# Adding the output-projection bias on GpSimd in pieces of one row block instead of one instruction

## What is computed

```python
x = x + attn(_layernorm(x))            # ... y @ Wo.T + bo
x = x + xattn(_layernorm(x), ctx)      # ... out @ W_out.T + b_out
x = x + ffn(_layernorm(x))             # fake-quantized silu(gate) * up, down
```

## Time and profile before

| | us |
|---|---|
| median of 3 runs | 990.71 (989.15 to 991.78) |
| the profiled execution, its own time | 986.81 |
| its span in the trace | 985.1 |
| POOL busy | 313.9 (32% of the span) |
| the nine bias instructions of line 679 | 36.4 of those |

### The profile page before, as it was taken

How to read it: one execution, slowest core, us unless ns; L and a number is a source line. 1 busy time by engine, 2 the same in 40 slices (tenths; PEclk the granted TensorE clock), 3 DMA queues, 4 the chain that set the end, 5 groups by cost and what they waited for, 6 DMA issues and landing times. The chain is left out here.

```text
span 985.1 us, 17246 instructions
## 1 busy us (share of the span) xinstructions
PE 899.3 (91%) x6003; PEld 440.0 (45%) x6018; DVE 710.8 (72%) x1467; ACT 601.1 (61%) x1118; POOL 313.9 (32%) x348
## 2 busy tenths in 40 slices
PE   4788999999999989999999999999999998988976
PEld 2433443455544534464446343554444454543344
DVE  3889866768766783777777928777674568778977
ACT  2335577746576577447675775456788624637974
POOL 1351135330431218413431165313512122203723
PEclk9979999999999999999999999999999999999999
DMA  5340111335222142101220313202210243115009
GB/s 164 108 124 17 56 58 53 76 60 82 82 77 73 43 146 76 55 17 56 92 88 17 126 45 99 63 31 82 87 49 2 86 150 100 37 38 171 1 9 184
DMA packets 83568, 73.42 MB, mean 75 GB/s; under 512 B 19244, under 2 KB 79788, under 8 KB 83484
## 3 DMA queue, kind: packets, MB, share of 16 engines
q1 hardware_dynamic: 75772, 66.17, 22.2%
q0 software_dynamic: 4256, 3.21, 2.6%
q10 hardware_dynamic: 3456, 2.94, 1.0%
HBM read 19.81 MB, written 13.13 MB: 33 GB/s over the span
## 5 line engine op out<-in xcount | busy, mean ns | idle before, releaser
L767 ACT ACTIVATE probs<-psum 128x512 f32<-128x512 f32 (+1 forms) x608 | 314.6, 577 | 179.5 <-PE psum L962 176.6
L1136 DVE CUSTOM_DVE_ANT_0 junk<-psum,mask 128x640 bf16<-128x640 f32 (+3 forms) x256 | 253.4, 1022 | 59.4 <-PE psum L926 57.2
L684 POOL TENSOR_SCALAR_AFFINE_SELECT probs<-probs 128x512 f32<-128x512 f32 x128 | 81.6, 640 | 391.5 <-ACT probs L767 391.2
L962 PE MATMUL psum<-q_stack,k_stack 98*128 98x512 bf16 (+3 forms) x768 | 188.0, 331 | 6.7 <-DMA q_stack<-max_rows 2.6
L987 PE MATMUL psum<-probs,v_sb 128*17 128x512 f32 (+3 forms) x1536 | 158.9, 492 | 3.8 <-POOL probs L684 3.4
L1132 DVE TENSOR_REDUCE rowmax<-psum 128x4 f32<-128x512 f32 (+2 forms) x96 | 97.3, 1045 | 62.9 <-PE psum L920 62.5
L926 PE MATMUL psum<-k_stack,q_stack 96*128 96x512 bf16 (+3 forms) x512 | 128.7, 344 | 5.8 <-DVE rowmax L1136 4.5
L962 PEld LDWEIGHTS psum<-q_stack,k_stack 98*128 98x128 bf16 x768 | 62.7, 98 | 136.6 <-ACT probs L767 80.9
L886 PE MATMUL psum<-xnT,wT 128*128 128x512 f32 x192 | 90.8, 604 | 0.6 <-ACT xnT L732 0.5
L811 PE MATMUL psum<-wT,xnT 128*128 128x256 f32 x384 | 87.6, 385 | 0.4 <-ACT xnT L732 0.3
L811 PEld LDWEIGHTS psum<-wT,xnT 128*128 128x128 f32 x384 | 73.3, 193 | 12.6 <-ACT xnT L732 1.2
(11 more groups left out here) (180 smaller groups left out, 1242.7 us busy)
## 6 DMA issues: line engine op xcount, KB each, us to landing
q_stack<-q_parts SPq DMA_DIRECT2D x192, 64.0 KB, 2.6
k_stack<-k_parts SPq DMA_DIRECT2D x192, 64.0 KB, 2.6
xq_stack<-xq_parts SPq DMA_DIRECT2D x168, 64.0 KB, 2.6
xn<-in_x SPq DMA_DIRECT2D x8, 512.0 KB, 5.0
res<-in_x SPq DMA_DIRECT2D x4, 1024.0 KB, 6.8
out<-res SPq DMA_DIRECT2D x8, 512.0 KB, 2.9
normT_hbm<-xnT SPq DMA_DIRECT2D x6, 512.0 KB, 3.9
xf<-normT_hbm SPq DMA_DIRECT2D x6, 512.0 KB, 3.7
```

Of the source, the lines that this page charges most:

```text
L684: nc.gpsimd.affine_select(out=tile, in_=tile, compare_op=ALU.is_ge, fill=0.0, base=0, pattern=[[0, GH], [1, P]], channel_multiplier=-1).th ...
L767: nc.scalar.activation(probs[n % 2][:, heads * k:heads * k + heads, 0:cols], bank_a(s)[:, 0:heads * cols].rearrange("p (h n) -> p h n", h= ...
L962: last = nc.tensor.matmul(bank[:, cols * n:cols * n + cols], k_stack[:, slot, h, P * j:P * j + P], q_stack[:, slot, half, h, q0 - HALF * h ...
L1136: nc.vector.tensor_tensor_reduce(out=junk[D_STEPS.place(s) % 2][:, 0:keys], in0=bank_d(s)[:, 0:keys], in1=m.mask[:, T - keys:T], scale=1.0 ...
```

## The change

POOL's one `tensor_tensor` for a `bias` step becomes a loop over its row blocks, one instruction of 128x256 each: eight where the step covers the batch, four in the two steps of batch 3. Only the last one of a step raises `biased`. There is no wait between the pieces. What is added, the tiles and the order of the steps stay.

```diff
                     bias = m.bias_f[(1, 3)[layer]][:, :].unsqueeze(1).to_broadcast([P, 4 * len(halves(part)), C])
-                    nc.gpsimd.tensor_tensor(rows, rows, bias, ALU.add).then_inc(biased, 1)
+
+                    for t in range(4 * len(halves(part))):
+                        last = nc.gpsimd.tensor_tensor(rows[:, t, :], rows[:, t, :], bias[:, t, :], ALU.add)
+                    last.then_inc(biased, 1)
```

## The result

The changed kernel is slower: 996.78 us median of 20 runs (992.22 to 1001.77) against 991.91 of 20 runs of the kernel before (986.33 to 998.04), ratio 1.0041, 95% interval 1.0024 to 1.0058 (the quotient of the two medians is 1.0049, within it). The profiled execution took 1001.77 us, at the slow end of its 20 runs, its span 1000.0. The forecast was 1.6 us less and the range ended at 993.6.

The account below looks back on a forecast made before the run. PE was busy 91% of the span, DVE 72%, POOL 32%, so POOL's work counts only through who waits. Terms -0.4 - 1.2 + 0 = -1.6 us gave 989.1 us, range 987.2 to 993.6.

Parts of the forecast that it names:

- The price of a piece: POOL's bias adds: 736 ns for 256 columns, eight pieces 5.54 us, POOL about 8 us busier.
- Nobody waits for POOL: Behind all nine biases, the next users of POOL's work have enough slack for its longer steps: cost 0.
- One link gets through at each boundary: Behind the first bias, eight linked DVE instructions pass eight POOL pieces, one for each piece: gain 0.4 us.
- The first stall: DVE line 1052 beside the bias of 70.75 us, 4.90 us long: -0.4 us forecast.
- the second: DVE line 1151 at 851.84 us beside the last two biases, 2.33 us long: PE gets back 1.2 us.
- rival 1: POOL doesn't let go between pieces: +1.0 at the first place, +0.85 at the last, sum +1.9, 992.6 us; chance 0.25.
- the trace agrees: Shared port of DVE and POOL: whoever starts first holds it for the whole instruction; 4.90 us against 4.51.
- rival 2: As rival 1, and TensorE's clock falls once more behind the first bias, 1.7 us: sum +3.6, 994.3 us; chance 0.08.
- Rival 3: Links hardly held by pieces: -2.1 us at the first bias, -1.2 at the last two, sum -3.3, 987.4; chance 0.12.
- The base: Median of the three runs before, 3.9 us above the profiled execution of 986.81, from which the 1.6 was taken.

Follow-up runs that it names:

- The middle alone: Against the kernel before, pieces in the six middle bias steps only, the first and the last two whole: ratio 1.0010.
- the unread matmuls: Changed kernel plus matmuls whose results nobody reads, put into TensorE's waits behind the two held DVE instructions: 1.0016 to the kernel before; that kernel filled likewise: 1.0004.
- the moved kernels: Against the kernel before, first and last bias start later, away from the DVE links: 0.9937 with whole biases, 0.9956 with pieces.
- the half pieces: Each piece of the change cut once more, 16 of 128x128 for a batch, no wait between: 1.0065 to the kernel before.

## Why the prediction was wrong, step by step

*The price of a piece*: 736 ns forecast, 721 measured; a train of eight 5.54 us forecast, 5.48 to 5.51 measured; POOL 8 us busier forecast, 7.7 by the groups. Right.

*Nobody waits for POOL*: right as far as the runs tell. The middle alone gives 1.0010 (0.9984 to 1.0035), and the stretches around its biases are as long as before (88.4 us).

*One link gets through at each boundary*: this is the step that failed. The first stall grew by 0.97 us (5.87 for 4.90, PE idle 2.90 for 1.91) where -0.4 was forecast, the second by 0.82 (3.15 for 2.33, PE idle 2.03 for 1.20) where -1.2 was. Not one of the seven boundaries was open. The mistake was to read from rows 6 how POOL's next instruction takes the port: there, nothing was queued on POOL. The row that showed a queued one was in rows 3, and the prediction used it only for rival 1: line 1052, issued 0.36 us ahead of the bias, lost against it. Its sizes, +1.0 and +0.85, are those measured. It should have had the larger chance, since every piece but the first is queued and nothing showed DVE getting in between two adds in succession. That such a hold would pass on to the time of its stage was right: 0.9 and 0.8 us.
The Trainium skill (GPSIMD Engine Reference, Instruction dispatch) says that GpSimd's cores go on to the next instruction with no barrier; the traces agree, as the trains have no gap (eight pieces of 721 ns take 5.48 us). The Trainium skill (SBUF — State Buffer, Who interferes with whom) has the port held for one whole instruction; here the 5.87 us show it held for a whole row of queued ones, and the measurement decides. The prediction's "the trace agrees" covered only the length of the hold: by the recorded starts the link, at 70.39, was ahead of the bias, at 70.75, and yet it was the one held.

*And the clock*: rival 2 put one fall more, 1.7 us, at a chance of 0.08. Nine traces have the pieces queued in the first step, and all nine have half clock in stage 2: 0.8 us with the unread matmuls, 1.7 to 5.4 in the others. Of the eight traces in which the first hold is as before or gone, seven have none; the exception is the one of the last two steps only (6.8). The price was 1.3 to 1.6 us in the change, 20.0 to between 21.3 and 21.6. "The 1.91 us of idling there now cost no clock" was true, and said nothing about 2.90.
Over all runs the change has a mean clock of 0.9796 (44 runs), the kernel before 0.9820 (126). The share of the time at half level is twice what the mean clock lacks to 1; that is 40.7 against 35.8 us. A microsecond at half level costs about half a microsecond at most (stage 3 of the kernel before took 13.5 us with 3.4 at half level and 11.9 with none): at most 2.4. With the holds, 0.97 + 0.82 + 2.4 = 4.2; measured 4.1 in the first comparison and 4.7 and 5.1 in the two others. That the sum fits doesn't prove the clock's part. Within the 126 runs of the unchanged kernel a microsecond more at half level goes with only 0.37 us more of time, and at that price the sum is 3.6. And the kernel with pieces in the first step has the half clock of stage 2 in both its traces, but mean clocks of 0.9821 and 0.9812, close to those of the kernel before. So of the 4 to 5 us the holds' 1.8 are shown by the traces; the rest goes with a lower mean clock, and what brings it stays open.

*Rival 3*: nothing of it; no link of 0.17 among the pieces. Its price for stalls that are gone, 2.1 and 1.2 us, was right: the moved kernels show 2.1 and 1.3.

*The base*: the median of three runs, 990.71, was 1.2 us below that of twenty, 991.91. Rival 2's price, +3.6, on that gives 995.5; the measured 996.78 lay 1.3 us above that. Three runs that span 2.6 us said little of the scatter: the twenty span 11.7.

*The range*: it ended at rival 1 with 1 us for scatter and left rival 2 out; rivals 1 and 2 and the base together come to 995.5 of the 996.78.

## What to carry to other kernels

Cutting a POOL instruction into pieces didn't let VectorE in between them here as long as the next piece stood ready in POOL's queue (but for the last boundary of the half pieces, in two places of three); it only makes the hold longer, by 0.14 us for each piece more (trains of 5.49 for 4.51 with eight, 6.61 with sixteen). What opens the boundaries is a semaphore wait of POOL between pieces (0.9952 here), and what needs no pieces at all is to let the long instruction start beside VectorE work that it doesn't hold, such as row maxima read from PSUM (0.9937). Before a hold is priced away, look in the trace for a row in which the instruction that is to let go has a successor queued behind it.

## What the runs showed of the hardware that was not expected

- Between two pieces with a wait between them two VectorE links of 128x8 get through, one of 0.17 us and one of 0.58 that ends with the next piece; the forecast had one a piece.
- With pieces of 128x128 the 15th of 15 boundaries was open in the first and the last place, and those before it that the link met were closed; in the third place with a held instruction, at 527.19, it was closed. No run tells why.
- The same kernel takes 986.8 to 999.5 us, over 126 runs. Falls of TensorE's clock of 3.4 us, or twice or three times that where they follow one another, come at places that differ from run to run (53.5, 70.6, 101.3, 261.8, 954.7 and 982.0 us in the first trace of the kernel before; 32.8, 56.6, 73.7, 264.9, 694.9, 858.8 and others in the second), 36 us at half level in the mean. With the change, which lengthens TensorE's idle time by a microsecond in two places, that mean is 5 us higher; that the one brings the other isn't shown.
